# Head outputs and softmax shifts turned by VectorE in 32x32 blocks, and two PSUM banks that change places at each head

## What is computed

```python
Q, K, V = (split into heads of (x @ W.T + b))            # 2 sequences x 16 heads, each 2048 x 16
A = softmax(Q @ K.T / sqrt(16))                          # per head 2048 x 2048
A_stable = 0.6 * A + 0.4 * L                             # L: a fixed band of +-3 tokens
out = (A_stable @ V) joined over heads, @ Wo.T + bo
```

## Time and profile before

| what | value |
|---|---|
| median of 3 runs | 1990.95 us (1990.76 to 1991.04) |
| profiled execution, span from first to last instruction | 2006.8 us |
| attention heads, first scores to last values | about 125 to 1426 us of the span |
| one head | 40.65 and 40.75 us in turn |
| TensorE busy over the span | 1951.3 us (97%) |
| VectorE busy | 1626.5 us (81%) |
| ScalarE busy | 1374.2 us (68%) |
| GpSimd busy | 346.9 us (17%) |
| granted TensorE clock over the span | 0.995 |

### The profile page before, as it was taken

The page is one execution under the profiler, slowest core; times in us unless marked ns, Lnnn a source line. Parts: engine busy times, 40 slices in busy tenths (PEclk is TensorE's granted clock), DMA queues, the critical chain, the costliest instruction groups (busy, mean ns, idle before and its releaser), DMA issues. The chain is left out here.

```text
span 2006.8 us, 47862 instructions
## 1 busy us (share of the span) xinstructions
PE 1951.3 (97%) x16384; PEld 1036.7 (52%) x16384; DVE 1626.5 (81%) x2075; ACT 1374.2 (68%) x2471; POOL 346.9 (17%) x379
## 2 busy tenths in 40 slices
PE   7999999999999999999999999999998799999997
PEld 3543333333333333333333333333687689999997
DVE  6799999999999999999999999994255565555564
ACT  3358888888888888888888888889544422233332
POOL 1361010001000100001000100010024532232233
PEclk9999999999999999999999999999999899999999
DMA  7954355335643454336534554341123677788884
GB/s 266 245 111 92 78 102 115 74 74 97 108 90 74 90 99 106 74 80 102 113 74 74 100 105 90 74 93 54 42 74 131 242 235 227 245 269 297 263 272 113
DMA packets 105849, 264.09 MB, mean 132 GB/s; under 512 B 20896, under 2 KB 52768, under 8 KB 99104
## 3 DMA queue, kind: packets, MB, share of 16 engines
q1 hardware_dynamic: 92624, 245.29, 48.6%
q0 software_dynamic: 13152, 17.83, 4.6%
HBM read 206.95 MB, written 73.94 MB: 140 GB/s over the span
## 5 line engine op out<-in xcount | busy, mean ns | idle before, releaser
L626 DVE TENSOR_REDUCE part_max<-psum 128x1 f32<-128x1024 f32 x1024 | 1240.8, 1222 | 50.6 <-PE psum L750 37.7
L681 ACT ACTIVATE probs<-psum 128x512 f32<-128x512 f32 x2048 | 1111.1, 596 | 145.4 <-PE psum L763 78.2
L763 PE MATMUL psum<-score_q,score_k 50*128 50x512 f32 x2048 | 745.9, 446 | 0.1
L750 PE MATMUL psum<-max_k,max_q 48*128 48x512 f32 x2048 | 737.9, 449 | 0.5 <-DVE part_max L626 0.4
L775 PE MATMUL psum<-probs,v_ones 128*32 128x256 f32 x8192 | 654.1, 391 | 9.4 <-ACT heads_sb L696 9.0
L763 PEld LDWEIGHTS psum<-score_q,score_k 50*128 50x128 f32 x2048 | 306.9, 184 | 404.7 <-ACT probs L681 390.7
L775 PEld LDWEIGHTS psum<-probs,v_ones 128*32 128x32 f32 x8192 | 162.1, 107 | 380.8 <-issue 198.1
L750 PEld LDWEIGHTS psum<-max_k,max_q 48*128 48x128 f32 x2048 | 294.2, 185 | 12.8 <-issue 7.0
L1184 ACT ACTIVATE x_sb<-psum,x_sb 128x512 f32<-128x512 f32 (+1 forms) x160 | 101.6, 636 | 257.8 <-PE psum L1564 243.1
L1583 PE MATMUL psum<-w,h_hi 128*128 128x256 f32 x1120 | 202.1, 279 | 2.7 <-DVE h_lo L1385 2.5
L1583 PEld LDWEIGHTS psum<-w,h_hi 128*128 128x128 f32 x1120 | 178.7, 189 | 13.8 <-DVE h_lo L1385 3.2
(11 more groups left out here) (185 smaller groups left out, 1352.3 us busy)
## 6 DMA issues: line engine op xcount, KB each, us to landing
w<-w_split SPq DMA_DIRECT2D x40, 2048.0 KB, 7.9
max_q<-qk_pieces SPq DMA_DIRECT2D x192, 128.0 KB, 7.2
score_k<-qk_pieces SPq DMA_DIRECT2D x192, 128.0 KB, 4.7
xs<-in_pads SPq DMA_DIRECT2D x33, 528.0 KB, 8.3
qk_pieces<-pieces SPq DMA_DIRECT2D x32, 512.0 KB, 4.6
w_split<-w_pair SPq DMA_DIRECT2D x32, 512.0 KB, 8.8
max_k<-qk_pieces SPq DMA_DIRECT2D x192, 64.0 KB, 8.2
score_q<-qk_pieces SPq DMA_DIRECT2D x192, 64.0 KB, 2.2
```

Source lines behind the costliest of these rows:

```text
L626: nc.vector.tensor_reduce(part_max[:, t, p:p + 1], ps_m[p].rearrange("q b f -> q (b f)"), axis=AXIS.X, op=ALU.max).then_inc(m_read, 1)
L681: nc.scalar.activation(probs[kb % 2][:, chunk * BLOCK:(chunk + 1) * BLOCK], bank_of(at), ACT.Exp, scale=float(HD) ** -0.5).then_inc(exp_do ...
L750: last = nc.tensor.matmul(ps_m[p][:, h, :], max_q[u][rows, t * P:(t + 1) * P], max_k[u][rows, p * BLOCK:(p + 1) * BLOCK], start=True, stop ...
L763: nc.tensor.matmul(bank_of(at), score_k[u][rows, kb * P:(kb + 1) * P], score_q[u][rows, part * BLOCK:(part + 1) * BLOCK], start=True, stop ...
```

## The change

Transposes no longer run on TensorE. VectorE turns 32x32 blocks in place of a full 128x128 transpose. For that to give the right layout, the queries of a sequence are stored in quarter order: quarter j of the 2048 positions holds those tokens that lie in the j-th group of 32 of their tile of 128. The projection's query matmul reads the tokens in that order, and the store puts four pieces of 128 positions instead of one run of 512 (keys stay as they were).

The head output: after key block 1 VectorE turns `heads_sb` to `heads_tok`, after key block 2 it inverts the sums. The shift: after key block 12 VectorE turns `shift` to `shift_row`, now 128 rows of 32, and SyncE waits for VectorE. `load_shift` makes eight DMAs, each of 16 rows of 128 bytes, into pieces of two rows of `score_q`. The two copies on ScalarE and the transposes on TensorE are gone, and with them the two extra units in the score ring.

The output bank is bank 2 for even heads and bank 3 for odd ones; in key block 0 a head's scores still use the old ring, from key block 1 on a ring with the other of the two banks. The first values of a head no longer wait for the copy; the third score of key block 1 does, and the second one waits for a bank used two units before.

```diff
-                            dst = dram["qk_pieces"][qk, head:head + HEADS // KD, :, :, ds((n % BPS) * BLOCK, BLOCK)]
-                            sp.dma_start(dst.rearrange("h d c t -> (h d) c t"),
-                                         pieces[u][:, qk, m, :, :].bitcast(F32)).then_inc(stored[u], 16)
+                            rows = dram["qk_pieces"][qk, head:head + HEADS // KD, :, :, :]
+                            rows = rows.rearrange("h d c t -> (h d) c t")
+                            src = pieces[u][:, qk, m, :, :].bitcast(F32)
+                            if qk == 0:
+                                dst = rows.rearrange("p c (j n) -> p c j n", j=BPS)[:, :, :, ds((n % BPS) * P, P)]
+                                src = src.rearrange("p c (j n) -> p c j n", j=BPS)
+                            else:
+                                dst = rows[:, :, ds((n % BPS) * BLOCK, BLOCK)]
+                            sp.dma_start(dst, src).then_inc(stored[u], 16)
...
-                                                    xnT[:, ds(n, 1), k, :].squeeze(1),
+                            rows = xnT[:, ds(n, 1), k, :].squeeze(1)
+                            if qk == 0:
+                                rows = rows.rearrange("p (b j r) -> p j b r", b=BT, j=BPS)
+                            done = nc.tensor.matmul(ps_qk[j], w["qk"[qk]][:, k, m * P:(m + 1) * P], rows,
...
+    FIRST_RING, RING_OF, OUT_OF = ((0, 1, 2), (1, 0, 3)), ((1, 0, 3), (0, 1, 2)), (2, 3)
+
+    def s_done(n, kb, c):
+        return n * UNITS + CH * kb + c + 1
+
+    def score_bank(u, kb, c):
+        at = CH * kb + c
+        return psum[:, FIRST_RING[u][at % RING] if at < CH else RING_OF[u][(at - CH) % RING], :]
+
+    def out_bank(u):
+        return psum[:, OUT_OF[u], :]
+
+    SHIFT_DMAS = ROW_TILES * P // QUAD
...
         def load_shift(u):
+            n = PIECES * ST // ROW_TILES
             for h in range(ROW_TILES):
-                for c in range(PIECES):
-                    row, first = h * ROW_TILE + STACK + c, c * ST + h * ST // ROW_TILES
-                    sp.dma_start(score_q[u][row:row + 1, :].bitcast(F32).rearrange("o (t q) -> o t q", q=P),
-                                 shift_row[first:first + ST // ROW_TILES, :].bitcast(F32)).then_inc(shift_in[u], 16)
+                row = h * ROW_TILE + STACK
+                dst = score_q[u][row:row + PIECES, :].bitcast(F32).rearrange("c (t q) -> c t q", q=P)
+                for q in range(P // QUAD):
+                    sp.dma_start(dst[:, :, q * QUAD:(q + 1) * QUAD],
+                                 shift_row[q * QUAD + h * n:q * QUAD + (h + 1) * n, :]).then_inc(shift_in[u], 16)
...
-                    sp.wait_ge(exp_done, count_of(shift_unit(n)))
+                    sp.wait_ge(shift_turned, n + 2)
                     load_shift(1 - u)
...
             pool.wait_ge(shift_step, m + 1)
-            if m == 1:
-                pool.wait_ge(first_tr, 1)
-            elif m > 1:
-                pool.wait_ge(s_ready, count_of(shift_unit(m - 2)))
-            nc.gpsimd.tensor_copy(shift[:, 0, :], neg_max[:]).then_inc(shift_hi, 1)
+            pool.wait_ge(shift_turned, m)
...
+        def turn_shift(m):
+            dve.wait_ge(shift_ready, m + 1)
+            nc.vector.transpose(shift_row[:], shift[:].rearrange("p h c t -> p (h c t)").bitcast(F32)
+                                ).then_inc(shift_turned, 1)
+
+        def turn_heads(n):
+            dve.wait_ge(o_copied, n + 1)
+            if not isinstance(n, int) or n > 0:
+                dve.wait_ge(tok_used, n)
+            nc.vector.transpose(heads_tok[:].rearrange("p t e -> p (t e)"), heads_sb[:]).then_inc(heads_turned, 1)
+
         def invert(n):
-            tok = heads_tok[:].rearrange("p (c b e) -> p c b e", c=BT, b=BPS)
-            inv = inv_sum[:].rearrange("p (c b) -> p c b", c=BT)
-            dve.wait_ge(exp_done, count_of(heads_unit(n)))
-            nc.vector.reciprocal(inv, tok[:, :, :, HD]).then_inc(inv_ready, 1)
+            dve.wait_ge(heads_turned, n + 1)
+            nc.vector.reciprocal(inv_sum[:], heads_tok[:, :, HD]).then_inc(inv_ready, 1)
...
+        turn_shift(0)
...
-                    if kb == HEADS_AT + 1:
+                    if kb == TURN_AT:
+                        turn_heads(n)
+                    if kb == INVERT_AT:
                         invert(n)
                     if ahead == ST - 1 and not (last and u):
                         split_shift(n + 1)
+                    if kb == SHIFT_AT and not (last and u):
+                        dve.wait_ge(shift_in[u], 16 * SHIFT_DMAS * (i + 1))
+                        turn_shift(n + 1)
 
         twice(dve, pairs, body)
-        dve.wait_ge(last_copied, 1)
-        tok = heads_tok[:].rearrange("p (c b e) -> p c b e", c=BT, b=BPS)
-        nc.vector.reciprocal(inv_sum[:].rearrange("p (c b) -> p c b", c=BT), tok[:, :, :, HD]).then_inc(inv_ready, 1)
+        turn_heads(NHEADS)
+        invert(NHEADS)
...
-        def copy_shift(at):
-            act.wait_ge(s_ready, count_of(at))
-            nc.scalar.activation(shift_row[:], bank_of(at)[0:PIECES * ST, 0:P], ACT.Copy).then_inc(exp_done, 1)
-
-        def copy_tok(n):
-            if not isinstance(n, int) or n > 0:
-                act.wait_ge(tok_used, n)
-            act.wait_ge(s_ready, count_of(heads_unit(n)))
-            nc.scalar.activation(heads_tok[:], bank_of(heads_unit(n)), ACT.Copy).then_inc(exp_done, 1)
-
-        def copy_o(n):
+        def copy_o(n, u):
+            act.wait_ge(heads_turned, n + 1)
             act.wait_ge(pv_done, ST * (n + 1) + PV_OPEN)
-            nc.scalar.activation(heads_sb[:], ps_o, ACT.Copy).then_inc(o_copied, 1)
+            nc.scalar.activation(heads_sb[:], out_bank(u), ACT.Copy).then_inc(o_copied, 1)
...
-                    if kb == HEADS_AT:
-                        copy_tok(n)
-                    if kb == SHIFT_AT and not ends:
-                        act.wait_ge(shift_in[u], 16 * SHIFT_DMAS * (i + 1))
-                        copy_shift(shift_unit(n))
+                        copy_o(n, u)
 
         twice(act, pairs, body)
-        act.wait_ge(last_tr, 1)
-        act.wait_ge(tok_used, NHEADS)
-        nc.scalar.activation(heads_tok[:], ps_tr, ACT.Copy).then_inc(last_copied, 1)
...
+        def scores(n, kb, u, c):
+            if kb == 1 and c == RING - 1:
+
+                pe.wait_ge(o_copied, n + 1)
+            else:
+
+                held = 2 if kb == 1 and c == 1 else RING
+                if not isinstance(n, int) or s_done(n, kb, c) > held:
+                    pe.wait_ge(exp_done, s_done(n, kb, c) - held)
...
+        def values(n, kb, u, part):
 
             if part == 0:
-                pe.wait_ge(exp_done, count_of(unit(n, kb, CH - 1, ends)))
-                if kb == 0:
-                    pe.wait_ge(o_copied, n + 1)
+                pe.wait_ge(exp_done, s_done(n, kb, CH - 1))
...
-                    if kb == HEADS_AT:
-                        wait_bank(heads_unit(n))
-                        pe.wait_ge(o_copied, n + 1)
-                        transpose_heads(bank_of(heads_unit(n))).then_inc(s_ready, 1)
-                    if kb == SHIFT_AT and not ends:
-                        wait_bank(shift_unit(n))
-                        wait_apart(pe, count, shift_ready, n + 2, ones_set, POOL_SET)
-                        transpose_shift(bank_of(shift_unit(n))[0:PIECES * ST, 0:P]).then_inc(s_ready, 1)
...
-        pe.wait_ge(o_copied, NHEADS + 1)
-        transpose_heads(ps_tr).then_inc(last_tr, 1)
...
-                                     ("shift", [P, PIECES, ST], F32R), ("shift_row", [PIECES * ST, P], F32R)):
+                                     ("shift", [P, ROW_TILES, PIECES, ST // ROW_TILES], F32R),
+                                     ("shift_row", [P, PIECES * ST], F32)):
```

More of the change, by code:

```diff
@@ L399, in attend @@
     psum = keep["psum"]
-    ps_s = [psum[:, c, :] for c in range(3)]
-    ps_o = psum[:, 3, :]
     ps_m = [psum[:, 4:6, :], psum[:, 6:8, :]]
-    ps_tr = psum[:, 7, :]
-    ps_shift = ps_s[2][0:PIECES * ST, 0:P]
     CH = BPS
@@ L408, in attend @@
     RING = 3
-    UNITS = CH * ST + 2
-    HEADS_AT = 1
-    def unit(n, kb, c, ends=False):
-        after = (kb > HEADS_AT + 1) + (kb > SHIFT_AT + 1 and not ends)
-        return n * UNITS, CH * kb + c + after
-    def heads_unit(n):
-        return n * UNITS, CH * (HEADS_AT + 2)
-    def shift_unit(n):
-        return n * UNITS, CH * (SHIFT_AT + 2) + 1
-    def count_of(at):
-        return at[0] + at[1] + 1
-    def bank_of(at):
-        return ps_s[at[1] % RING]
-    SHIFT_DMAS = PIECES * ROW_TILES
+    UNITS = CH * ST
+    TURN_AT, INVERT_AT = 1, 2
+    FIRST_RING, RING_OF, OUT_OF = ((0, 1, 2), (1, 0, 3)), ((1, 0, 3), (0, 1, 2)), (2, 3)
[7 more added lines that the diff above has]
+    SHIFT_DMAS = ROW_TILES * P // QUAD
     PARTS = 2
@@ L469, in v_tiles_before @@
         return spread if half < FIRST_SCORES else min(TILES, TILES - 2 + half - FIRST_SCORES)
```

(48 more changed lines are left out.)

51 lines of the change are left out of this document (18 added, 33 removed).

## The result

| | before | after |
|---|---|---|
| median of the runs | 1990.86 us (1990.43 to 1991.04, 4 runs) | 2250.59 us (2231.47 to 2263.41, 4 runs) |
| ratio to before, 95% interval | | 1.129 [1.123, 1.136] |
| profiled execution, span | 2006.8 us | 2261.6 us |
| mean granted TensorE clock over the span | 0.995 | 0.876 |
| TensorE / VectorE / ScalarE busy | 97 / 81 / 68% | 95 / 73 / 60% |

The change made the kernel 260 us slower. The forecast was 2049 us with a range up to 2075, so the direction was right and the size was not: some 200 us are missing from the sum.

The account below looks back on a forecast made before the run. TensorE's order of work was taken as the bound. Heads 0 to 29 at +1.93 us (+58), head 30 -0.9, head 31 -0.7, beginning +1.5 and +0.8 made +58.6: 2049 us, range 1977 to 2075.

Parts of the forecast that it names:

- the clock falls as well: Rival, chance 0.08: TensorE's idle stretch in attention drops its clock; 2065 at one head in three, 2098 at each.
- Shift load: Before a head's last key block: eight DMAs issued by SyncE land late, so TensorE stalls 2.86 us a head.
- c: Time per shift DMA issue on SyncE: 0.70 us taken, 0.36 to 0.89 possible, break-even at 0.42.
- queue rule: Shift DMAs: queues used are the largest number up to 16 dividing both outermost sizes; 8 before, 2 after, issue still slow.
- Gain of a head: TensorE per head: transposes and copy wait go, -1.13 us; a bank wait and VectorE's turn add 0.10 each.
- three long half steps: TensorE in each head, lengthened by copy wait, head output transposes and shift transpose: 0.34, 0.58, 0.21 us too long.
- VectorE's turns: Transposes moved to VectorE: 0.69 us for the head output (0.45 to 1.22), 0.19 for the shift.
- Beginning: Before and in the first head: smaller query-store pieces cost +1.5 us, the first shift load +0.8 net.

Follow-up runs that it names:

- run with two queues: Changed kernel, turn after key block 12, with four of the eight shift DMAs issued by GpSimd on its own queue: 1975.74 us, ratio 0.992.
- the filler: Three unread full-size FP32 matmuls of 512 columns a head, put in the changed kernel ahead of the wait for the shift load: 2045.11 us, ratio 1.027.
- run with 48-row work: Changed kernel with four unread FP32 matmuls of 512 columns on 48 array rows behind each head's key block 15: 2499.69 us, ratio 1.254.

## Why the prediction was wrong

The step that failed is the price of the rival "the clock falls as well", and with it its chance. The sum had the clock full in attention, at no cost, and the rival had 1.6 us a fall; by the runs a fall costs 7.8 us, and it came at every one of the 30 waits.

- *Clock.* The prediction had the mechanism and gave it 0.08; it is what happened, at all 30 waits. It priced a fall at 1.6 us, read from a single stretch of the routing stage. There the clock is back in 3.4 us, and the matmuls of that row take 128 rows. A second look at that stage would have said the same: the changed kernel's own routing stage, in the very execution whose attention loses the clock for 18.2 us at a time, has it back after 3.4:

```profile
1822.40:1825.80 3.40, 3.40 (x9) 2.62 (x9) 2.48 (x10) 0.69 (x1) 2.83 (x3) 0.50 0.99 325
1825.80:1840.00 14.20, 12.75 (x72) 9.74 (x72) 8.47 (x38) 9.44 (x12) 9.62 (x10) 1.00 1.02 376
```

In attention a fall lasted 18.2 us on average, which costs 18.2 x 0.43 = 7.8 us, five times as much. Even with a fall at each head the priced rival stopped at 2098; with 7.8 it would have come to 2049 + 30 x 7.8 = 2283. The chance lay between one row at which the clock fell and one at which it held, both of the routing stage; no row of before showed an idle stretch of that length in attention, and there it fell each time.
- *Shift load.* Right. c is 0.67 (0.70 taken, bounds 0.36 to 0.89), the wait 2.3 to 2.5 us at heads 0 to 29 (2.86 forecast for the same heads, none for head 30), ended by the shift's load, the eight issues in 5.27 us (5.5 forecast). The run with two queues shows that it was the issues and not the transfers. The queue rule of the Trainium skill (DMA: Bandwidth & Descriptors, "Why a DMA increments its semaphore by 16 and not by 1"), from which the prediction took the slow kind of issue for both shapes, is in line with this: the new shape's median issue is 0.611 us, the old one's was 0.634. No run parts that rule from the other differences between these DMAs and the loads from DRAM, so why the issue is slow stays open.
- *Gain of a head.* Right. -1.13 + 0.10 + 0.10 = -0.93 was forecast for a head without the late load; with the load on time a head takes 39.78 us, against 40.65 and 40.75: -0.92. The three long half steps are gone, and two are left that are longer than 1.24 us, both where the prediction had them. One takes 1.43, 0.19 more where 0.10 was forecast: the second score of key block 1 waits for the exponential before it, which ends at 447.72 + 1.09 = 448.81. The other, behind VectorE's turn, takes 1.30 to 1.32. The bank of the old output is free in time, as forecast: the copy ends at 448.69 + 0.60 = 449.29, the third score comes at 449.85. TensorE and ScalarE in the run with the turn between the reductions of key block 11:

```profile
448.42 0.50 PE L759 MATMUL psum<-score_q,score_k 50*128 50x512 f32 x1
...
448.86 0.49 PE L759 MATMUL psum<-score_q,score_k 50*128 50x512 f32 x1
...
449.85 0.50 PE L759 MATMUL psum<-score_q,score_k 50*128 50x512 f32 x1
```

```profile
447.72 1.09 ACT L698 ACTIVATE probs<-psum 128x512 f32<-128x512 f32 x2 [0.15 <-PE psum L759]
448.69 0.60 ACT L704 ACTIVATE heads_sb<-psum 128x512 f32<-128x512 f32 x1
```

- *VectorE's turns.* Right: 0.70 and 0.20, against 0.69 and 0.19 by the nearest rows.
- *Beginning.* A little too dear. +1.5 for the query stores and +0.8 for the first head were forecast; the first scores come at 124.70 against 124.69, with a wait of 0.31 for their load.

Together: without the clock's fall the changed kernel would take about 2035 us (2045 less the 10 us that the filler is longer than the wait), where the sum said 2049; the wait of 2.42 for 2.86 is 13 of the 14 us between. The rest, some 215 us of the median, is the clock (229 in the profiled execution, which is longer). The range ended at 2075 since it took the rival's price as known, while it rested on one row of another stage.

## What to carry to other kernels

When a change lets TensorE wait, the wait is not its own price: here 2.4 us of waiting a head cost 1.5 us net of the gain, and the clock behind it 7.8 us more. Price a fall by matmuls like those that will run behind it, and where the profile has no such stretch leave the upper end open. And before a load is cut into more pieces, count the issues on its queue against the slack at its consumer; here starting it 3.4 us earlier turned a loss of 13% into a gain of 1.5%.

## What the runs showed that was not expected

- The half clock can last long while TensorE is never idle: 47.82 us without a break in the run with 48-row work.
- The same wait of 1.2 to 1.4 us cost the clock at 7 heads and not at 23 others of one execution, and a fall can begin some 2 us after the wait has ended.
- Work that nobody reads made the kernel faster: some 110 us of long 128-row matmuls behind the wait won 46 us net, and three of them a head inside the wait won 205.
- Twenty-four short matmuls more in a loop's body brought a fetch of code and a gap of 3.2 to 3.8 us at its return; six long ones brought none.
